# Cross-attention and quantised FFN on one core: the FFN written out pair by pair, its down products up to nine pairs behind, scale and clip later in their queues

## What is computed

```python
def _mx_linear(x, w):
    return jnp.einsum('bsh,oh->bso', _q_act(x), _q_w(w))
...
gate = _mx_linear(x, w_gate)          # 512 -> 2048
up = _mx_linear(x, w_up)
inter = jax.nn.silu(gate) * up
return _mx_linear(inter, w_down)      # 2048 -> 512
...
x = x + _L0_xattn_ref(_layernorm(x, axis=-1), ctx_2048, ...)
x = x + _L0_ffn_ref(_layernorm(x, axis=-1), ...)
```

## Time and profile before

| | us |
|---|---|
| median of 3 runs | 2055.06 (2054.39 to 2056.13) |
| profiled execution, its own time | 2054.62 |
| its span in the trace | 2053.1 |
| PE busy over the span | 2019.0 (98%) |
| DVE busy | 1534.7 (75%) |
| ACT busy | 999.6 (49%) |
| POOL busy | 739.8 (36%) |

### The profile page before, as it was taken

The page is one execution under the profiler, slowest core; times in us unless marked ns, Lnnn a source line. Parts: engine busy times, 40 slices in busy tenths (PEclk is TensorE's granted clock), DMA queues, the critical chain, the costliest instruction groups (busy, mean ns, idle before and its releaser), DMA issues. The chain is left out here.

```text
span 2053.1 us, 45755 instructions
## 1 busy us (share of the span) xinstructions
PE 2019.0 (98%) x15430; PEld 1503.3 (73%) x15430; DVE 1534.7 (75%) x3339; ACT 999.6 (49%) x2683; POOL 739.8 (36%) x882
## 2 busy tenths in 40 slices
PE   8999999999999999999999999999999999999997
PEld 6888878788888887878888888888888874444443
DVE  6767777877777777777777777775666558888886
ACT  8955555445555454555555555555555452223222
POOL 5422232323233233323333333231111006777776
PEclk9999999999999999999999999999999999999999
DMA  8834444444445444444444445443333273454554
GB/s 256 212 72 84 86 93 84 93 88 88 88 89 91 91 91 85 89 91 91 91 87 88 87 91 88 91 86 75 68 67 70 55 173 79 79 87 87 89 87 79
DMA packets 455038, 193.26 MB, mean 94 GB/s; under 512 B 418400, under 2 KB 431200, under 8 KB 454848
## 3 DMA queue, kind: packets, MB, share of 16 engines
q1 hardware_dynamic: 432496, 139.26, 35.2%
q0 software_dynamic: 16016, 45.23, 9.3%
q10 hardware_dynamic: 6336, 6.29, 1.0%
HBM read 61.21 MB, written 27.26 MB: 43 GB/s over the span
## 5 line engine op out<-in xcount | busy, mean ns | idle before, releaser
L1094 PE MATMUL b_qk<-kvT,attn_weights 128*128 128x256 f16 x3072 | 377.2, 273 | 3.7 <-DVE qk L763 2.9
L1094 PE MATMUL b_qk<-xT,attn_weights 128*128 128x256 f16 x3072 | 377.2, 273 | 0.0
L1094 PE MATMUL b_v<-attn_weights,kvT 128*128 128x256 f16 x3072 | 377.2, 273 | 0.0
L654 ACT ACTIVATE prob<-b_s,nmax 128x256 f32<-128x256 f32 x514 | 238.8, 469 | 278.2 <-DVE nmax L924 276.4
L1094 PEld LDWEIGHTS b_qk<-kvT,attn_weights 128*128 128x128 f16 x3072 | 299.9, 98 | 93.2 <-issue 5.1
L951 DVE SCALAR_TENSOR_TENSOR psplit<-prob,rrec,psplit 128x256 f16<-128x256 f32 x514 | 306.0, 636 | 79.5 <-ACT psplit L664 79.5
L763 DVE SCALAR_TENSOR_TENSOR qk<-b_qk,qk 128x512 f16<-128x512 f32 x256 | 176.5, 690 | 246.6 <-ACT qk L610 236.1
L610 ACT ACTIVATE qk<-b_qk 128x512 f16<-128x512 f32 x256 | 152.4, 595 | 425.2 <-PE b_qk L1094 424.9
L1094 PEld LDWEIGHTS b_v<-attn_weights,kvT 128*128 128x128 f16 x3072 | 300.2, 98 | 35.1
L1094 PEld LDWEIGHTS b_qk<-xT,attn_weights 128*128 128x128 f16 x3072 | 300.2, 98 | 35.1
L664 ACT ACTIVATE psplit<-prob,rrec 128x256 f16<-128x256 f32 x514 | 233.1, 500 | 68.1 <-DVE rrec L944 68.1
(11 more groups left out here) (132 smaller groups left out, 2635.7 us busy)
## 6 DMA issues: line engine op xcount, KB each, us to landing
ffn_w<-wffn SPq DMA_DIRECT2D x48, 256.0 KB, 2.8
acc<-xtok POOLq DMA_DIRECT2D x16, 512.0 KB, 4.9
out<-acc POOLq DMA_DIRECT2D x16, 512.0 KB, 3.3
xrow<-xtok POOLq DMA_DIRECT2D x31, 256.0 KB, 3.2
out<-attn_weights POOLq DMA_DIRECT2D x31, 256.0 KB, 4.5
kvrow<-kvt POOLq DMA_DIRECT2D x61, 128.0 KB, 2.4
stage<-wattn SPq DMA_DIRECT2D x12, 512.0 KB, 4.4
ffn_scratch<-ffn_t SPq DMA_DIRECT2D x48, 128.0 KB, 2.4
```

What stands on the lines that cost most here:

```text
L654: last = eng.activation(half(prob, q, 256), half(bS, q, 256), ACT.Exp, bias=nmax[:, q:q + 1], scale=1.0, accum_out=rsum[:, q:q + 1])
L1094: last = eng.matmul(out, l, r, start=(a == 0), stop=(a == len(pairs) - 1))
```

## The change

- The FFN stage is written out for all 64 pairs; the loops and the constant `STRAIGHT` go.
- There are twelve slots for transposed pairs instead of four (`inner_t`; the eight new ones lie where attention weights were).
- `down` of pair d is issued behind the units of pair d + 3 at first, but none is issued at pairs 34, 38, 42, 46, 50 and 54, so from pair 55 on it is nine pairs behind, and nine of them (`BEHIND`) stand after the last unit. The `move_down` and `add_out` that belong to them move too.
- On DVE `clip` of the pair before stands after both `inner` of a pair, not between them.
- On ACT `scale` of the pair before stands between the two `silu`; it stood behind both, for the pair itself. `i_scale` gets a second buffer, so `scale` waits for the `rescale` of two pairs before, not of the one before.
- The last pair is transposed by DMA like the others; PE's transposes, the copies behind them and the bf16 identity go.

```diff
-STRAIGHT = 18
+INNER_SLOTS = 12
+NO_DOWN = (0, 1, 2, 34, 38, 42, 46, 50, 54)
+DOWN_AT = {v: d for d, v in enumerate(v for v in range(PAIRS) if v not in NO_DOWN)}
+MOVE_AT = {v: d // 2 for v, d in DOWN_AT.items() if d % 2}
+BEHIND = range(len(DOWN_AT), PAIRS)
...
-        iqT = free_part(2, 1, 4, 4).bitcast(BF16)
+        inner_t = [free_part(2, 1, 4 + a, 1).bitcast(BF16) for a in range(4)]
+        inner_t += [free_part(3, 0, a, 1).bitcast(BF16) for a in range(8)]
...
-        i_scale = sb("inner_scale", 32, BF16)[:, :]
+        i_scale = sb("inner_scale", 2 * 32, BF16)[:, :]
...
-                if not isinstance(v, int) or v >= 4:
-                    wait_apart(eng, "down_done", v - 3)
-                eng.dma_start_transpose(half(iqT, at, 1024).rearrange("p (j f) -> p j f", j=8),
-                                        half(iq, at % 2, 1024)).then_inc(sm[f"iqT_loaded{at}"], 16)
...
+                if v == PAIRS - 1:
+                    wait_apart(eng, "last_q", 1)
+                if v >= INNER_SLOTS:
+                    wait_apart(eng, "down_done", v - INNER_SLOTS + 1)
+                eng.dma_start_transpose(inner_t[v % INNER_SLOTS].rearrange("p (j f) -> p j f", j=8),
+                                        half(iq, v % 2, 1024)).then_inc(sm["inner_loaded"][v % INNER_SLOTS], 16)
+
+            for v in range(PAIRS):
+                transpose_inner(v)
+                if v % 2 == 0 and v // 2 + 2 < TILES:
+                    load_x_tile(v // 2 + 2, v // 2 % 2)
...
+                if v - 1 in MOVE_AT:
+                    add_out(MOVE_AT[v - 1], MOVE_AT[v - 1] % 2)
+
+            for v in range(PAIRS):
+                pair(v)
...
+            for t in range(TILES - 1):
+                if t not in [MOVE_AT.get(v - 1) for v in range(PAIRS)]:
+                    add_out(t, t % 2)
...
-                if not isinstance(v, int) or v > 0:
-                    eng.wait_ge(sm["i_q"], v)
-                eng.activation(i_scale, i_pow, ACT.Copy, scale=16.0).then_inc(sm["i_scale_done"], 1)
-
-            def tile(t, at, begun=0, out_=True):
-                for h in range(2):
-                    for k in (2 * h, 2 * h + 1):
-                        if k >= begun:
-                            silu(t, k)
-                    if out_ and h == 0:
-                        move_down(t - 2, at)
-                    scale(2 * t + h)
-
-            tile(0, 0, begun=2, out_=False)
-            tile(1, 1, out_=False)
-            tile(2, 0)
-            tile(3, 1)
-            with eng.Fori(2, TILES // 2) as m:
-                for a in range(2):
-                    tile(2 * m + a, a)
-            move_down(TILES - 2, 0)
-            eng.wait_ge(sm["last_tr"], 1)
-            eng.activation(half(iqT, 6), pLast[0], ACT.Copy).then_inc(sm["last_moved"], 1)
+                if v >= 2:
+                    eng.wait_ge(sm["i_q"], v - 1)
+                eng.activation(half(i_scale, v % 2, 32), i_pow, ACT.Copy, scale=16.0).then_inc(sm["i_scale_done"], 1)
+
+            for v in range(PAIRS):
+                for k in range(2 * (v % 2), 2 * (v % 2) + 2):
+                    if v > 0:
+                        silu(v // 2, k)
+                    if v > 0 and k % 2 == 0:
+                        scale(v - 1)
+                if v in MOVE_AT:
+                    move_down(MOVE_AT[v], MOVE_AT[v] % 2)
+            scale(PAIRS - 1)
+            for t in range(TILES - 1):
+                if 2 * t + 1 in BEHIND:
+                    move_down(t, t % 2)
...
-            def tile(t, at, begun=0, last_batch=False):
-                for h in range(2):
-                    v = 2 * t + h
-                    if 2 * h >= begun:
-                        inner(t, 2 * h)
-                    if h == 1:
-                        clip(t, at, 0)
-                    elif not (isinstance(t, int) and t == 0):
-                        clip(t - 1, 1 - at, 1)
-                    if 2 * h >= begun:
-                        inner(t, 2 * h + 1)
-                    reduce(v, h)
-                    scales(v)
-                    round_a(v, h)
-                    if last_batch and v == 0:
-                        add_rows(B - 1, 0)
-                        add_rows(B - 1, 1)
-                    if last_batch and v in LAST_STEPS:
-                        last_step(*LAST_STEPS[v])
...
+                t, h = v // 2, v % 2
+                if v > 0:
+                    inner(t, 2 * h)
+                    inner(t, 2 * h + 1)
+                    clip(v - 1)
+                reduce(v, h)
+                scales(v)
+                round_a(v, h)
+                if v == 0:
+                    add_rows(B - 1, 0)
+                    add_rows(B - 1, 1)
+                if v in LAST_STEPS:
+                    last_step(*LAST_STEPS[v])
+
+            for v in range(PAIRS):
+                pair(v)
+            clip(PAIRS - 1)
...
+            def down(d):
+                t, h = d // 2, d % 2
+                rows = inner_t[d % INNER_SLOTS]
+                eng.wait_ge(sm["inner_loaded"][d % INNER_SLOTS], 16 * (d // INNER_SLOTS + 1))
+                if d == 0:
+                    eng.wait_ge(sm["down_resident"], 16 * 4)
+                    eng.wait_ge(sm["o_added"], 2 * B)
...
-            def tile(t, at, begun=0):
-
-                for h in range(2):
-                    for k in (2 * h, 2 * h + 1):
-                        if k >= begun:
-                            gate_up(t, k, at)
-                    if not isinstance(t, int) or t - 2 + h >= 0:
-                        down(t - 2 + h, (at + h) % 2, 1 - h)
-
-            tile(0, 0, begun=3)
-            eng.wait_ge(sm["down_resident"], 16 * 4)
-            eng.wait_ge(sm["o_added"], 2 * B)
-            tile(1, 1)
-            tile(2, 0)
-            tile(3, 1)
-            with eng.Fori(2, TILES // 2) as m:
-                for a in range(2):
-                    tile(2 * m + a, a)
-            down(TILES - 2, 0, 1)
-            down(TILES - 1, 1, 0)
-            for j, (ready_, value) in enumerate((("i_q", PAIRS), ("last_q", 1))):
-                eng.wait_ge(sm[ready_], value)
-                for c in range(4):
-                    last = eng.transpose(pLast[j][:, c * P:(c + 1) * P], half(iq, 2 + j)[:, c * P:(c + 1) * P],
-                                         identb[:, :])
-                last.then_inc(sm["last_tr"], 1)
-            down(TILES - 1, 1, 1, last=True)
+            for v in range(PAIRS):
+                for u in range(2 * v, 2 * v + 2):
+                    if u >= 3:
+                        gate_up(u // 4, u % 4, u // 4 % 2)
+                if v in DOWN_AT:
+                    down(DOWN_AT[v])
+            for d in BEHIND:
+                down(d)
```

More of the change, by code:

```diff
@@ L398, in _ @@
             eng.memset(ident[:, :], 0.0).then_inc(sm["ident_ready"], 1)
-            eng.memset(identb[:, :], 0.0).then_inc(sm["ident_ready"], 1)
             eng.memset(powers[:, 0:1], -0.5).then_inc(sm["ident_ready"], 1)
             eng.memset(powers[:, 1:2], 1e-5).then_inc(sm["ident_ready"], 1)
[L402 to L405, removed]
+            eng.wait_ge(sm["ident_ready"], 3)
+            eng.affine_select(out=ident[:, :], in_=ident[:, :], compare_op=ALU.not_equal, fill=1.0, base=0,
+                              pattern=[[-1, P]], channel_multiplier=1).then_inc(sm["ident_ready"], 1)
             for z in (qk, probT, vbuf):
@@ L568, in add_out, with pair @@
                               accum_op=ALU.add).then_inc(sm[f"out_stored{at}"], 16)
-            def tile(t, at, out_=True, last_batch=False):
-                for h in range(2):
-                    v = 2 * t + h
-                    if not (isinstance(v, int) and v == 0):
-                        rescale(v - 1, 1 - h)
-                    round_b(v, h)
-                    if last_batch and v == 0:
-                        store_x1(B - 1, acc[:, 0:2 * D].rearrange("p (t d) -> p t d", t=2))
-                    step = POOL_STEPS.get(v) if last_batch else None
-                    if step == "rstd":
-                        tile_rstd(B - 1)
-                    for j in range(2):
-                        if step == f"round{j}":
-                            x_round(TILES - 2 + j, j)
-                        if step == f"rescale{j}":
-                            x_rescale(TILES - 2 + j)
-                if out_:
-                    add_out(t - 2, at)
-            tile(0, 0, out_=False, last_batch=True)
-            tile(1, 1, out_=False, last_batch=True)
-            eng.wait_ge(sm["x1_stored"], 16 * B)
-            for t in range(2, STRAIGHT):
-                tile(t, t % 2, last_batch=True)
-            with eng.Fori(STRAIGHT // 2, TILES // 2) as m:
-                for a in range(2):
-                    tile(2 * m + a, a)
+            def pair(v):
+                if v > 0:
+                    rescale(v - 1, (v - 1) % 2)
+                round_b(v, v % 2)
+                if v == 0:
```

(24 more changed lines are left out.)

63 lines of the change are left out of this document (19 added, 44 removed).

## The result

The changed kernel takes 2069.61 us (median of 4 runs, 2069.02 to 2070.68); the kernel before, on the same chip, 2054.72 (4 runs, 2053.19 to 2056.13). The ratio is 1.0073, with a 95% interval of 1.0056 to 1.0091: slower by 14.9 us, between the bounds of 11.5 and 18.7. The profiled execution took 2070.68 with a span of 2068.7, against 2054.62 and 2053.1 before.

A forecast was written before the change was run, and what follows sets the result against it. Two nearly equal rings, DVE with POOL (5.12 us a pair) and PE's pair (5.195), were taken as the bound. Terms 5.9 - 0.3 - 0.8 + 0 + 4.5 + 1.8 = +11.1, plus 0.6, gave 2066.5 us; 8-in-10 range 2057 to 2072.

The forecast's parts named there:

- The ring stays at 5.12: DVE and POOL loop: `clip`, `rescale`, held power, inverse, rounding still take 5.12 us a pair; waiting becomes a longer power.
- the rival of a longer ring: Rival: two `inner` in a row cost 0.05 to 0.1 us more a pair, giving 2070 to 2073; chance 0.18.
- The steps lose their cover, +5.9: DVE's eleven last-batch steps, before partly covered by the 0.56 us wait at `clip`, cost full length: +5.9 us.
- The first pairs, +0.6: Start of the FFN stage: `clip` stands behind an `inner` that waits for `silu`, estimated at one step, +0.6 us.
- Scale with two buffers, -0.3: ACT, pair 10: `scale` no longer waits for a late `rescale`, 0.3 us back, bounds 0 and 3.0.
- Straight code, -0.8: FFN loop written out: straight pairs took 5.164 us, the loop's 5.195; over 27 pairs -0.8 us.
- Six moved `down`, 0: PE, middle pairs: the freed time is idle, since units wait for `inner`; gain 0, bound -10.4 us.
- The tail, +4.5 + 1.8: After the last unit: nine `down` precede the last, +4.5 us; pair 60's waits for tile 26's add and ACT's copy, +1.8.
- only the tail costs: Rival: PE slack absorbs the last-batch steps, or the last unit comes earlier; 2060 or 2056 us, chance 0.16.
- the ring gets shorter: Rival: `rescale` does not hold the power, or is held itself; a ring pair takes 4.56 us, time 2039; chance 0.09.

The follow-up runs named there:

- e4: Changed kernel with the block maxima and powers kept in PSUM, so power and inverse read PSUM, and scale waits for the inverse: 2050.03 us, ratio 0.9982 to before.
- e1: Changed kernel with only `clip` put back between the two `inner`: 2063.16 us, ratio 1.0041 to the kernel before.
- e3: Changed kernel without gaps: `down` issued behind every pair from pair 3 on, three behind the last unit: 2063.27 us, ratio 1.0044 to before.
- e2: Kernel before with only `clip` moved behind both `inner`: 2061.88 us, ratio 1.0037 to before.
- e5: Changed kernel with tile 30 added on DVE and stored by SP instead of added on POOL: 2067.3 us, ratio 1.0068 to before.
- e7: Changed kernel with power, inverse and `round_a` reading PSUM (a second inverse added) and tile 30 added on DVE: 2039.92 us, ratio 0.9948 to before.
- the five kernels without gaps: Variants of the changed kernel with `down` issued behind every pair from pair 3 on, some with other edits too: 2041.6 to 2063.3 us.
- e8: Changed kernel with `clip` back between the `inner` and `down` behind every pair from pair 3 on: 2056.22 us, ratio 1.0015 to before.

## Why the prediction was right or wrong, point by point

The forecast was +11.7 us (2066.5) and the measurement +14.9 (2069.6): sign and mechanism held, the size was 3.1 us short, inside the range. In the two traces, by which the points below go, the difference is 15.6, so the sum was 3.9 short: 2.1 at the very end, 0.7 in the tail, 0.4 up to pair 36, and 0.65 that is scatter. (The sum's last step is itself 0.2 short: 2066.3 and 0.4 make 2066.7.)

- **The ring stays at 5.12.** Right: 5.11. The step of 0.72 that I feared between two `inner` is 0.60, so the rival of a longer ring had the right time for another reason. e4 shows that the hold of the power is what keeps it at 5.12.
- **The steps lose their cover, +5.9.** Right in kind. The pair with the `apply` step went from 5.94 to 6.53, +0.59. Ten of the eleven pairs with a step grew by 0.44 to 0.59 and the other by 0.07, 5.6 in all, and e1 against the changed kernel prices the whole edit at 6.4.
- **The first pairs, +0.6.** Up to `reduce` of pair 3 the changed kernel takes 17.83 us instead of 16.13, +1.70. At the start `clip` delays `inner` and PE idles 2.43 us; its clock then falls:

```profile
1710.51 1.12 PE L1068 MATMUL b_pt<-attn_weights 128*128 128x512 bf16 x4 [2.43 <-DVE attn_weights L817]
1711.42 1.91 PE L1068 MATMUL b_x<-attn_weights 128*128 128x512 bf16 x4
1713.13 1.49 PE L1068 MATMUL b_qk<-attn_weights 128*128 128x512 bf16 x3
```

  Four matmuls take 1.91 us instead of 1.03, the granted clock from 1712 to 1716 is 0.66, and pair 2 to 3 takes 6.13 us instead of 5.12. e3 has the same code here and PE idles 2.44 us in the same place, but its granted clock stays full and that pair takes 5.12; its first three pairs cost +0.70. So the term was right but for the clock, and that microsecond is not in every execution.
- **Scale with two buffers, -0.3.** Small, as I took it: pair 10 to 11 went from 7.44 to 7.23, -0.2. Against e2, where `clip` has moved as well, it is -0.8.
- **Straight code, -0.8.** Measured -0.72 between pairs 36 and 63, in the changed kernel as a whole; no run isolates it.
- **Six moved `down`, 0.** Right: e3 has them back, and from `reduce` 36 to 63 it is 0.2 us longer.
- **The tail, +4.5 + 1.8.** The stop before pair 60's `down` is 1.62 us, the last `down` starts 0.7 us later than the sum would have it, and to DVE's last add it is +6.99 instead of +6.3. The chain began at 2040.50 instead of 2038.6. The experiments price the six `down` behind the last unit at 6.3 to 6.9.
- **The step that failed: where the kernel ends.** I summed to the last `down` and took what follows as unchanged. Before, POOL's last add was issued 3.2 us ahead of DVE's last add; now only 1.2 us, because ten `down` run to the end without a hole and tile 30's copy and add stand right before tile 31's. The end of the span is POOL's last add plus 10.1 us, its landing and the drain, and so it moved 2.1 us more than DVE's. The earlier trace rows show the `down` and the landing, but I had not looked for what ends the span. e5, with that add taken off POOL, got 2.9 us back.
- **0.65 us before `reduce` of pair 0** was in no term and needs none: kernels with the same code up to there differ by up to 1.7 us at this point.

Of the rivals, "only the tail costs" is refuted by e1 and e2, and "the ring gets shorter" by the 5.11 us. It did get shorter as soon as its condition held: in e4 and e7, where the power is not held, the shortest pairs take 4.6 and 4.2 us.

## What to carry to other kernels

When two queues wait for each other, a wait that you fill with work is not a gain until you have walked the new ring once round: here the idle 0.56 us moved into the length of a DVE operation that POOL held, and busy time looked better while the time was the same. An operation much longer than its like (1.05 us for 0.18) whose end falls on the end of an operation of another engine is probably held by it. Here a small operand put in PSUM freed it, and gave more than any of the reorderings tried. Work moved off a bound engine in the loop has to be done somewhere, so count what it costs at the end, and count up to the instruction from which the span really ends, not up to the last matmul.

## What I had not expected of the hardware

- The end of the span came 10.0 to 10.4 us after the issue of POOL's last output add in eight kernels: some 4 us to its landing and then a drain of 5.7 on POOL's queue. In the five kernels without gaps it came 2.4 us after SP's last store (e8: 2053.68 to 2056.1).
- TensorE's clock fell to its lower level in some tails and not in others: after 3.21 us of idle time in e3 (`down` 3.52 us), and after 2.91 in e8, where it fell during the next `down` (2.92 us) and stayed low to the end (the last `down` 3.60), but not in the kernel before, whose PE idled 3.30 us in the same place and took 1.90:

```profile
2041.46 1.90 PE L1217 MATMUL b_w<-attn_weights 128*128 128x512 bf16 x8 [3.30 <-DMA attn_weights<-attn_weights]
```

  At the start of the stage it was the same: after 2.43 or 2.44 us of idle time the clock fell in the changed kernel, e2 and e5, and not in e3. The length of the last idle stretch alone does not tell the cases apart; what does is left open.
- Beside a `rescale` of 1.9 us the same power took 1.05 us from SBUF and 0.20 from PSUM. `round_a` took 1.05 beside it with both inputs in SBUF and 0.69 with the small one in PSUM, and `round_b`, which POOL runs beside `round_a`, went from 1.48 to 1.05.
